# Two-layer graph network on one core: flags, carries and returned weights of the layer-0 softmax, and the split of 196 destination fetches

## What is computed

```python
edge_index = stack([src, dst])                    # 25000 edges, dst sorted; 100000 nodes, 64 features
h = maximum(layernorm(x), 0)
# layer 0, 4 heads
delta = proj[src] - proj[dst]                     # proj = h @ w_proj, per head
radial = delta . radial_score - scale * edge_weight
tangential = delta . tangential_score
out = sum over both of segment_sum(segment_softmax(logits, dst) * delta, dst)
x = x + h + nan_to_num(mean over heads of out) @ w_out
# layer 1, three rounds over x[row], x[col] with row = src, col = dst
mask = clip(sigmoid(MLP(x[row], x[col])) * 1.5 - 0.45, 0, 1)
vals = mask * d[row] * d[col]                     # d = clip(rowsum(mask) ** -0.5, 0, 10)
x_next = segment_sum(vals * x[col], row)
```

## Time and profile before

| | us |
|---|---|
| median of 3 runs | 2831.31 (2831.07 to 2831.59) |
| the profiled execution | 2831.4 |
| its span | 2829.6 |
| busy: PE / DVE / ACT / POOL | 1649.0 / 2091.3 / 1073.2 / 1905.7 |

### The profile page before, as it was taken

How to read it: one execution, slowest core, us unless ns; L and a number is a source line. 1 busy time by engine, 2 the same in 40 slices (tenths; PEclk the granted TensorE clock), 3 DMA queues, 4 the chain that set the end, 5 groups by cost and what they waited for, 6 DMA issues and landing times.

```text
span 2829.6 us, 32874 instructions
## 1 busy us (share of the span) xinstructions
PE 1649.0 (58%) x8788; PEld 1262.0 (45%) x8788; DVE 2091.3 (74%) x5660; ACT 1073.2 (38%) x2214; POOL 1905.7 (67%) x1896
## 2 busy tenths in 40 slices
PE   1135667676508888256666546746666655656663
PEld 0025666666405555145454334534444444434442
DVE  6766998899778999355655536979668889657775
ACT  0025666666304443033333334434444344442221
POOL 0037777777786766677777774767766477745776
PEclk9997877877558888577777767878888778876555
DMA  0023444444201111422222112333323333324443
GB/s 8 0 60 92 137 129 138 129 139 127 84 2 32 45 43 41 87 59 66 61 62 64 41 35 56 85 99 105 103 91 74 86 102 105 104 68 120 126 116 81
DMA packets 279791, 226.66 MB, mean 80 GB/s; under 512 B 161731, under 2 KB 209855, under 8 KB 279481
## 3 DMA queue, kind: packets, MB, share of 16 engines
q1 hardware_dynamic: 221113, 184.48, 23.1%
q0 software_dynamic: 58496, 40.08, 6.8%
HBM read 151.81 MB, written 84.50 MB: 84 GB/s over the span
## 4 chain that ended last, share of the span: by engine, by line
POOL 48%; DVE 18%; issue 18%; PE 7%; DVEq 6%; DMA 2%; SPq 1%; ACT 1%; POOLq 0%; ACTq 0%
POOL big L1096 14%; POOL G L1076 13%; POOL regs L1973 7%; POOL out L1103 7%; POOL regs L1982 6%; DVE den L1377 2%; DVE big L1706 2%; PE bank L1562 2%; DVE bank L836 2%; DVE big L1394 2%; DVEq L1705 1%; PE bank L994 1%; DVE bank L847 1%; DVE G L830 1%; DVEq L837 1%
## 5 line engine op out<-in xcount | busy, mean ns | idle before, releaser
L1096 POOL DMA_INDIRECT big<-layer_rows,late x392 | 401.0, 1023 | 152.0 <-issue 118.8
L1973 POOL DMA_INDIRECT regs<-in_x,G x200 | 202.2, 1011 | 234.8 <-DVEq L1825 174.2
L1562 PE MATMUL bank<-regs,SQ 99*128 99x256 bf16 x1308 | 228.7, 345 | 84.7 <-ACT SQ L1467 78.1
L1103 POOL DMA_INDIRECT out<-G,scat_i x196 | 195.7, 999 | 104.3 <-issue 61.6
L1982 POOL DMA_INDIRECT regs<-in_x,G x200 | 220.1, 1101 | 65.4 <-issue 60.3
L685 POOL DMA_INDIRECT x_after_layer<-big,scat_i x200 | 196.5, 983 | 84.3 <-issue 65.7
L1076 POOL DMA_INDIRECT G<-x_after_layer,own_i x196 | 199.9, 1020 | 70.2 <-issue 60.7
L1076 POOL DMA_INDIRECT G<-x_after_layer,far_i x196 | 197.8, 1009 | 65.8 <-issue 65.8
L1064 POOL DMA_INDIRECT late<-degree_factors,late x152 | 152.8, 1005 | 99.9 <-DMA degree_factors<-den 56.6
L1562 PEld LDWEIGHTS bank<-regs,SQ 99*128 99x128 bf16 x1308 | 153.9, 121 | 144.7 <-ACT SQ L1467 97.0
L439 PE MATMUL bank<-regs 128*128 128x128 f32 x784 | 135.9, 327 | 119.4 <-DVE den L397 118.7
(11 more groups left out here) (417 smaller groups left out, 5384.6 us busy)
## 6 DMA issues: line engine op xcount, KB each, us to landing
den<-in_x SPq DMA_DIRECT2D x96, 256.0 KB, 3.7
x_after_layer<-den SPq DMA_DIRECT2D x96, 256.0 KB, 2.1
regs<-x_after_layer SPq DMA_DIRECT2D x96, 256.0 KB, 2.8
out<-regs SPq DMA_DIRECT2D x96, 256.0 KB, 2.1
XC<-row_of_far_degree SPq DMA_DIRECT2D x109, 128.0 KB
layer_rows<-TS SPq DMA_DIRECT2D x98, 128.0 KB
regs<-sought SPq DMA_DIRECT2D x49, 196.0 KB
regs<-row_of_edge SPq DMA_DIRECT2D x75, 128.0 KB
```

The source lines that it names most:

```text
L1096: ahead(g, l, REVERSED, lambda u, l=l: g.indirect_dma_start(far[:, tile_of(u // C, u % C), :], None, xt_d[l - 1], bass.IndirectOffsetOnAxi ...
L1103: g.indirect_dma_start(out, bass.IndirectOffsetOnAxis(ap=scat_i[1][:, u:u + 1], axis=0), SUM[b][:, k, :], None, bounds_check=top, oob_is_e ...
L1562: ins = pe.matmul(bank[2 + 2 * b + k // 2][:, (k % 2) * 256:(k % 2) * 256 + 256], OH[b][0:RB1 + 1, k * P:(k + 1) * P], TAB[0:RB1 + 1, part ...
L1973: g.indirect_dma_start(GR[:, c % DEEP, k, 0, :], None, a["x"], bass.IndirectOffsetOnAxis(ap=own0[:, c * C + k:c * C + k + 1], axis=0), bou ...
```

## The change

It does the following:

- The flags "same node as the edge before" are stored as bf16 at the time of the sort (`run_d`, in place of the node numbers `node_d`) and loaded into `SAME` by one transfer, which SP issues before step 45 of the pairs. DVE makes `NEG`, the two end flags and the "whole partition is one run" flag (now a minimum) after the last pairs and before the last `scored`.
- The carries across partitions go through PE: columns are turned into rows by products with the identity, the row of carries back into columns by products with a 1x1.
- The 13 transposes and 26 DVE operations for the weights become 26 f32 products, accumulated in pairs, and two DVE copies.
- FETCHED is 20: 80 dst fetches on POOL and 29 look-ups, spread over the first 48 steps by `seeks`; `SQD` has two buffers. The cast of all 196 columns is on DVE after the loop.

```diff
+SPAN = NCH - 2
+PADS = (TS16 - T) * TE
-FETCHED = 24
+FETCHED = 20
-        NTROW = 128 + TS16 * 128 + 128
-        node_d = dram("tile_nodes", (2, NTROW))
+        run_d = dram("run_flags", (1, TS16 * TE + 1), BF16)
-        SAME = regs[:, 0:SCAN + 1]
+        SAME = regs[:, 1024:1024 + SCAN // 2 + 1].bitcast(BF16)[:, 0:SCAN + 1]
...
             for c in range(NCH):
+                if c == NCH - 5:
+                    sp.wait_ge(signal("g_own"), 40)
+                    sp.dma_start(SAME, at(run_d, 0, [[0, H8], [SCAN, HC], [1, SCAN + 1]])).then_inc(signal("scan_ids"), 16)
                 look_sp(sp, c + AHEAD + 2)
...
-            for h in range(H8):
-                rows = slice(h * HC, (h + 1) * HC)
-                sp.dma_start(IDS[rows, 1:SCAN + 1].rearrange("c (k e) -> c k e", k=KC),
-                             at(node_d, 128, [[KC * 128, HC], [128, KC], [1, TE]])).then_inc(signal("scan_ids"), 16)
-                sp.dma_start(IDS[rows, 0:1], at(node_d, TE - 1, [[KC * 128, HC], [1, 1]])).then_inc(signal("scan_ids"), 16)
-                sp.dma_start(IDS[rows, SCAN + 1:SCAN + 2], at(node_d, 128 + KC * 128, [[KC * 128, HC], [1, 1]])).then_inc(signal("scan_ids"), 16)
-            for n_ in range(2):
-                sp.wait_ge(signal("ends_up"), n_ + 1)
-                sp.dma_start(crow[0:1, 0:640], ccol[:, 0:5]).then_inc(signal("ends_row"), 16)
-                sp.wait_ge(signal("carry_row"), n_ + 1)
-                sp.dma_start(ccol[:, 5:7], carr[0:1, 0:256]).then_inc(signal("carry_col"), 16)
...
+        def seeks(c):
+            return range(min(c, SPAN) * len(LOOKED) // SPAN, min(c + 1, SPAN) * len(LOOKED) // SPAN)
...
         def row_carry(v, n_, is_max):
-            v.wait_ge(signal("ends_row"), 16 * (n_ + 1))
             v.memset(O, first)
-            v.tensor_tensor(A_[:, 0:m], lp[:, 1:128], full[:, 0:m], ALU.mult)
-            v.tensor_tensor(A2_[:, 0:m], ln_[:, 0:m], full[:, 1:128], ALU.mult)
+            v.tensor_copy(FULLR, full)
+            v.drain()
+            v.tensor_tensor(A_[:, 0:m], lp[:, 1:128], FULLR[:, 0:m], ALU.mult)
+            v.tensor_tensor(A2_[:, 0:m], ln_[:, 0:m], FULLR[:, 1:128], ALU.mult)
+            v.wait_ge(signal("ends_row"), n_ + 2)
...
-                v.tensor_tensor(B_[:, 0:m], lp[:, 1:128], last[:, 0:m], ALU.mult)
-                v.tensor_tensor(B2_[:, 0:m], ln_[:, 0:m], frst[:, 1:128], ALU.mult)
+                v.tensor_copy(B_[:, 0:m], lp[:, 1:128])
+                v.tensor_copy(B2_[:, 0:m], ln_[:, 0:m])
+                v.drain()
+                v.tensor_tensor(B_[:, 0:m], B_[:, 0:m], last[:, 0:m], ALU.mult)
+                v.tensor_tensor(B2_[:, 0:m], B2_[:, 0:m], frst[:, 1:128], ALU.mult)
...
-            v.wait_ge(signal("carry_col"), 16 * (n_ + 1))
+            v.wait_ge(signal("carry_col"), n_ + 1)
+            v.tensor_copy(ccol[:, 5:7], bank[2][:, 256:258])
+            v.drain()
...
+            v.wait_ge(signal("scan_ids"), 16)
+            v.tensor_copy(ccol[:, 2:3], SAME[:, 0:1])
+            v.tensor_copy(ccol[:, 3:4], SAME[:, SCAN:SCAN + 1])
+            v.tensor_reduce(ccol[:, 4:5], SAME[:, 1:SCAN], AX.X, ALU.min)
+            v.tensor_scalar(NEG, SAME, -1.0, -LOW, ALU.add, ALU.mult)
+            v.drain().then_inc(signal("ends_up"), 1)
             scored(NCH - 1)
...
-            v.wait_ge(signal("scan_ids"), 16 * 24)
-            v.tensor_tensor(SAME, IDS[:, 1:SCAN + 2], IDS[:, 0:SCAN + 1], ALU.is_equal)
-            v.tensor_tensor(ccol[:, 4:5], IDS[:, 1:2], IDS[:, SCAN:SCAN + 1], ALU.is_equal)
-            v.drain()
-            v.tensor_scalar(NEG, SAME, -1.0, -LOW, ALU.add, ALU.mult)
-            v.tensor_copy(ccol[:, 2:3], SAME[:, 0:1])
-            v.tensor_copy(ccol[:, 3:4], SAME[:, SCAN:SCAN + 1])
-            v.drain()
+            run_stored(v, RUN_A)
             v.wait_ge(signal("sm_in"), 4)
+            v.wait_ge(signal("ends_row"), 1)
...
-            for q in range(4):
-                n_ = min(4, KC - 4 * q)
+            for q, n_ in enumerate((8, KC - 8)):
                 v.wait_ge(signal("sm_back"), q + 1)
-                B = bank[4 + q % 2][0:TE, 0:n_ * P].rearrange("p (k r h c) -> p k r h c", r=2, h=HEADS, c=HC)
-                for k in range(n_):
-                    v.tensor_copy(BTv[0:TE, 4 * q + k], B[:, k, 0])
-                v.drain()
-                for k in range(n_):
-                    ins = v.tensor_tensor(BTv[0:TE, 4 * q + k], BTv[0:TE, 4 * q + k], B[:, k, 1], ALU.add)
-                ins.then_inc(signal("alpha_out"), 1)
+                B = bank[4 + q][0:TE, 0:n_ * F].rearrange("p (k h c) -> p k h c", h=HEADS, c=HC)
+                v.tensor_copy(BTv[0:TE, 8 * q:8 * q + n_], B)
...
+            pe.wait_ge(signal("ends_up"), 1)
+            for k in range(3):
+                ins = pe.matmul(bank[7][0:1, k * P:(k + 1) * P], ccol[:, 2 + k:3 + k], ident[:, :], start=True, stop=True)
+            ins.then_inc(signal("ends_row"), 1)
             pe.wait_ge(signal("sm_lg"), 1)
...
+            for n_ in range(2):
+                pe.wait_ge(signal("ends_up"), n_ + 2)
+                for k in range(2):
+                    ins = pe.matmul(bank[2][0:1, k * P:(k + 1) * P], ccol[:, k:k + 1], ident[:, :], start=True, stop=True)
+                ins.then_inc(signal("ends_row"), 1)
+                pe.wait_ge(signal("carry_row"), n_ + 1)
+                for k in range(2):
+                    ins = pe.matmul(bank[2][:, 256 + k:257 + k], carr[0:1, k * P:(k + 1) * P], ident[0:1, 0:1], start=True, stop=True)
+                ins.then_inc(signal("carry_col"), 1)
...
             for k in range(KC):
-                q = k // 4
-                if q >= 2 and k % 4 == 0:
-                    pe.wait_ge(signal("alpha_out"), q - 1)
-                ins = pe.transpose(bank[4 + q % 2][0:TE, (k % 4) * P:(k % 4 + 1) * P], SLk[:, k, :], ident[:, :])
-                if k % 4 == 3 or k == KC - 1:
+                o_ = bank[4 + k // 8][0:TE, (k % 8) * F:(k % 8 + 1) * F]
+                pe.matmul(o_, SLk[:, k, :], ident[:, 0:F], start=True, stop=False)
+                ins = pe.matmul(o_, SLk[:, k, :], SWAP[:, 0:F], start=False, stop=True)
+                if k in (7, KC - 1):
                     ins.then_inc(signal("sm_back"), 1)
...
-            for k in range(RING):
-                g.wait_ge(signal(f"ring{k}"), rows_in(k))
-            g.tensor_copy(far_i[:, 0:C * FETCHED], farf[:, 0:C * FETCHED])
-            g.drain().then_inc(signal("dst_done"), 1)
```

More of the change, by code:

```diff
@@ L629, in L0_sp @@
                     mask(c + 2)
-                if c % 2 == 0:
-                    seek_dst_sp(sp, c // 2 + 2)
+                for e in seeks(c):
+                    seek_dst_sp(sp, e + 2)
         WHELD = 32
@@ L700, in row_carry @@
         def row_carry(v, n_, is_max):
-            R = crow[0:1, 0:640].rearrange("o (q k) -> o q k", k=5)
-            last, frst, lp, ln_, full = [R[:, :, k] for k in range(5)]
+            last, frst = [bank[2][0:1, k * P:(k + 1) * P] for k in range(2)]
+            lp, ln_, full = [bank[7][0:1, k * P:(k + 1) * P] for k in range(3)]
             m = 127
@@ L863, in L0_dve @@
                     renew(i - 4)
-                if i >= 2 and i % 2 == 0 and i // 2 - 1 < len(LOOKED):
-                    seek_dst_dve(v, i // 2 - 1)
+                for e in seeks(i - 2) if i >= 2 else ():
+                    seek_dst_dve(v, e)
             v.drain()
-            lo = C * FETCHED
-            v.tensor_copy(far_i[:, lo:], farf[:, lo:])
+            for k in range(RING):
+                v.wait_ge(signal(f"ring{k}"), rows_in(k))
+            v.tensor_copy(far_i[:, :], farf[:, :])
             v.drain().then_inc(signal("dst_looked"), 1)
@@ L918, in L0_act @@
                 out_t(c)
-                if c % 2 == 0 and c // 2 < len(LOOKED):
-                    seek_dst_act(s_, c // 2)
+                for e in seeks(c):
+                    seek_dst_act(s_, e)
         def L0_pe(pe):
@@ L1006, in seek @@
             def seek(c):
-                if c % 2 == 0 and c // 2 < len(LOOKED):
-                    seek_dst_pe(pe, c // 2)
+                for e in seeks(c):
+                    seek_dst_pe(pe, e)
             staged(NCH, [(0, turn_weighed), (1, project), (3, out_proj), (2, seek)])
@@ L1186, in L1_dve @@
             v.drain().then_inc(signal("weights1_clear"), 1)
-            v.wait_ge(signal("dst_done"), 1)
             v.tensor_scalar(far_c, farf[:, :], 2.0, 1.0, ALU.mult, ALU.add)
@@ L1631, in _ @@
             sp.dma_start(at(rowe_d, 0, [[128, HT], [HT * 128, 2], [1, 128]]), EHR).then_inc(signal("row_out"), 16)
-            sp.dma_start(at(node_d, 128, [[128, HT], [HT * 128, 2], [1, 128]]), NTt[:, 0:2, :]).then_inc(signal("nodes_out"), 16)
+            sp.dma_start(at(run_d, 1, [[TE, HT], [HT * TE, 2], [1, TE]]), SM0[:, :, 0:TE]).then_inc(signal("nodes_out"), 16)
             sp.dma_start(at(same0_d, 1, [[128, HT], [HT * 128, 2], [1, 128]]), SM0).then_inc(signal("nodes_out"), 16)
```

(6 more changed lines are left out.)

15 lines of the change are left out of this document (7 added, 8 removed).

## The result

| | before | after |
|---|---|---|
| median, runs side by side on one chip | 2831.19 (2829.57 to 2833.05), 6 runs | 2822.15 (2816.32 to 2825.63), 6 runs |
| the profiled execution | 2831.4 | 2822.59 |
| its span | 2829.6 | 2820.7 |

The ratio is 0.9966 [0.9953, 0.9979]: faster by 9.0 us [5.9, 13.3]. The forecast was 2823.6 within 2818 to 2830, faster.

The account below looks back on a forecast made before the run. DVE was taken as the bound: when it begins the loop and how much it does there, with POOL catching up. Terms -10.2 - 3.0 - 2.1 + 4.1 - 1.5 + 4.0 + 1.0 = -7.7 gave 2823.6, range 2818 to 2830.

Parts of the forecast that it names:

- Flags early: Softmax before the loop: one early load replaces 24, so the first scan starts at 774.3, not 784.45: -10.2 us.
- Carries by PE: Softmax scans: first carry 4.5 us against 7.5 (-3.0), second 4.25 against 6.4 (-2.1).
- Halves added by PE: Weights turned back to tiles before the loop: 52 records where there were 13, 10.6 us against 6.5: +4.1.
- where the clock rises: 3.7 to 9.6 us of work: PE's 26 products: clock rises after that much work; the middle, 6.7, makes 27 records slow and 25 fast.
- the clock stays low to the loop: Rival: PE's clock stays low through the products (+6.8, no gain at the loop's start): -3.5 in all, 2827.9; chance 0.20.
- A warm PE at the loop's start: First two loop steps: if the products leave the clock high, their transposes run faster: -1.5 us (0 to -2.0).
- The look-ups: Loop: four more look-ups for sixteen fetches add +4.0 us of DVE work and +1.0 of waits (-3 to +8).
- the +1.0: Loop: DVE's added waits for PE from four more look-ups, at 0.43 us each, PE's idle being filled.
- falls less often in the loop: Rival: clock rises early (products +2.8) and falls less often as look-ups fill PE's gaps (waits -3): -13, 2818.4; chance 0.18.
- parts 4 and 5: Loop: -1.5 us from a warm PE at its start, and +4.0 work and +1.0 waits from four more look-ups.
- 16 fetches fewer on POOL: POOL before the scatters: free 20.8 us earlier, but its first rows come later than that, so worth nothing.
- priced each pass as a whole transpose: Rival for the 26 products: each f32 product costs four transposes, 25.6 us, +7.8 in all, 2839.2; chance 0.02.

Follow-up runs that it names:

- g5_loadlate: The changed kernel with the one load of flags issued after the last dense stores and the mask made after the logits' copy: 2826.87, ratio 0.9979 to before.
- f10_dmacarry: The changed kernel with the carries across partitions by transfers again, as in the kernel before: 2832.96, ratio 0.9991 to before.
- f3_turned: The changed kernel with 13 transposes again instead of 26 f32 products, DVE copying and adding groups of four tiles: 2818.92, ratio 0.9945 to before.
- f9_only_lookups: The kernel before with only the split changed, 80 fetches and 29 look-ups over 48 steps: 2834.40 against 2835.03, ratio 0.9995.
- g7_best20: f3_turned with the mask made after the logits' copy: 2818.87, ratio 0.9944 to the kernel before.
- f1_even24: The changed kernel with its split undone, 96 fetches and 25 look-ups, one in every second step: 2826.06, ratio 0.9972 to before.

## Why the prediction was right, and where it was not

The sum was near and the direction right, though two of its terms were missed, in ways that nearly cancel.

1. *Flags early: right.* From the last operation of the pairs to the first scan 22.42 became 12.24, the 10.2 of the forecast. The minimum took 1.85 (1.8 forecast) and the mask 1.00 (1.01). The heading "flags early" names the lesser half: g5_loadlate and SP's queue show that 8.1 of it is one transfer for 24, and 2.1 the early issue.

2. *Carries by PE: right.* 4.57 and 4.29 against 4.5 and 4.25; the trip back waits 1.13, where the earlier trace rows have 0.94 and 1.1 was taken. Undone in f10_dmacarry: 4.7.

3. *Halves added by PE: right sign, size missed.* From the end of the division to the copy for the weighing (L822) 6.51 became 12.33: +5.8, not +4.1. The step that failed is "where the clock rises: 3.7 to 9.6 us of work". It was read from the loop, and here 52 records back to back held the engine 11.35 of 11.40 us at a granted 0.50 to the end. The reading of 3.7 also began its count at 855.90 and left out what PE had done just before it. Between 847.40 and 852.2 it worked 3.56 us on the 13 transposes, these being the last five:

```profile
850.23 1.12 PE L973 MATMUL bank<-ident,regs 128*126 128x128 f32 x4 [0.86 <-DVE den L817]
851.75 0.47 PE L973 MATMUL bank<-ident,regs 128*126 128x128 f32 x1 [0.41 <-DVE den L817]
```

All 13 were slow, and so were the loop's first two groups behind them (1.97 and 1.89 for eight). The rival "the clock stays low to the loop" was right for this part. Its price of +6.8 was high, since a record took 0.2135 here, where the rows have 0.246, and that for records of 128 and of 64 columns alike; these runs don't show why. The low-clock case was given 0.20, too little. The 0.50 of the earlier trace rows did not speak strongly for it, as PE had nothing to do in those two stretches; the slow transposes of the very stage that was to change did.

4. *A warm PE at the loop's start: failed.* -1.5 was forecast; the way from the first weighing to the first scan over segments went from 7.03 to 8.16, +1.1. The first two groups of transposes are slow and so is the first L1003 in its greater part (3.01, where the next take 1.93). The clock rose only at about 851, some 6 us after the loop's first transpose. From that transpose to the first group of eight at the high clock it is 5.5 to 6.7 us with the 26 products ahead (six kernels) and 5.4 to 6.4 with 13 transposes ahead (before, f3_turned, f9_only_lookups, g7_best20). So the products' work brought the rise no earlier.

5. *The look-ups: cost right, waits wrong.* DVE's work rose by 3.7 (4.0 forecast). The waits were to rise by 1.0 and fell from 10.8 to 3.6. The step that failed is the +1.0, taken from the mean wait for each look-up as if waits came with look-ups. They come with slow spells of PE's clock: of the 10 waits before, 9 stand within 5 us behind a slow group of w_out products, in f1_even24 all 8, in the change 3 of 4. And those spells are fewer with 29 look-ups: the second half of the rival "falls less often in the loop" was right, its first half (clock early) false. Together the loop gave -1.4 from first weighing to last scatter, where parts 4 and 5 were to give +3.5.

6. *16 fetches fewer on POOL: nothing, right.* POOL waits for DVE 44.2 us in the change, and f1_even24, with the 16 fetches back and the four look-ups gone, has a ratio within 0.0006 of the change's.

7. *Not foreseen:* the last scores came 0.5 earlier than before in spite of the mask, since the pairs ended 1.5 earlier. No part of the change bears on that. Over all these kernels the last scores start between 763.5 and 768.7, so it lies within the scatter between executions and chips.

The balance on the trace: -1.5 (pairs) - 10.2 - 3.0 - 2.1 (carries) + 5.8 (products) + 0.4 (a gap of issue of 0.43 between the second scan and the end copies, and roundings) makes -10.6 at the first weighing; -1.4 in the loop; +3.0 of scatter after it: -9.0, against the 8.9 that the span shows. That the forecast came within 1.5 us of the measured median is in part luck. At the first weighing it had -11.2 where -10.6 was measured, and 1.5 of that is scatter of the pairs. The loop came out 4.9 better than forecast (-1.4, not +3.5), and the 3.0 of scatter behind it hid part of that.

On the f32 product, the Trainium skill ("FP8 and Floating Point Precision", TensorE Precision Notes) says that true FP32 takes four passes. The prediction priced each pass as a whole transpose; the trace shows 0.427 a product, less than two of the low clock's transposes (0.246 each), so that price falls. Counted in columns it is the other way round: 0.427 × 1200 / 64 is 8.0 cycles for each column, where four passes of one cycle each (an estimate from that rule of the Trainium skill) would be four. PEld, the weight load, is busy 11.16 of the 11.40 us, and a record of 64 columns (0.2135) is hardly shorter than one of 128 (0.234 in f3_turned). So it seems that the weight loads, two to a product, fill the time and the columns hide in them; no run varied the columns alone to show it. For 512 columns the rule of the Trainium skill does nearly fit:

```profile
860.63 1.90 PE L1003 MATMUL bank<-den,wm 128*64 128x512 f32 x4
```

Two products, 1.90 at the high clock: 0.95 × 2400 / 512 is 4.45 cycles for each column.

**What stays open.** Why four more look-ups keep the clock up when 25 moved apart hardly do. From the first weighing to the last scatter PE's idle times of 1.9 us and more are 14 in the change and 15 before, so the longest gaps are not what went. Look-ups alone (f9_only_lookups) gain 3.4 in the loop and show nothing in the total. In its trace the last scores come 3.7 later than before, but that is another chip, where they start at 765.2 to 768.7 in all four kernels; a gain of 3.4 in whole times is below what its interval can tell. What PE's weight loads have to do with the 0.50 during the products is not tried either. Not tried: 13 f32 products with the sum of identity and SWAP as the moving matrix, which would add the halves in 26 records, 5.6 us by the 0.2135 measured, still more than the 3.04 of the transposes, though with two copies instead of eight operations on DVE.

## What to carry to other kernels

Price PE's work in a stretch of low granted clock as low to its end, unless a row of that same stretch shows a rise: here 26 products took 11.4 us of it, and the way to the loop was 6.4 shorter with 13 transposes and eight copies and adds on DVE. Where an engine waits for many small transfers of one array, first count them and read the issuing engine's queue: 24 transfers took SP 13.6 us to issue, one in their place gave 8.1, and issuing it early only 2.1 more. And a change of several parts should be undone part by part: here one of its parts cost 6 us of the 15 that two others brought.

## What was not expected of the hardware

- 52 f32 records back to back, 11.35 us busy of 11.40, left the granted clock at 0.50; the loop's mixed work raised it some 6 us after its start.
- 24 transfers on SP's queue went out 0.57 us apart, 13.6 us in all, and DVE went on 1.9 us behind the last.
- The loop's clock goes with the number of look-ups: 0.84 and 0.85 with 25, 0.89 to 0.91 with 29, 0.90 with 33. DVE's waits for them fall from 8.6 to 10.8 down to 2.1 to 5.1 us.
- One load of 128 rows of 3.3 KB took 6.1 us from issue to use after the pairs (g5_loadlate), with the dense rows' stores already landed and only POOL's fetches beside it.
- The 9.62 us of issue before the first scatter came when POOL made the cast (0.26 us) and its drain just before it. With the same 96 fetches and the cast on DVE (f1_even24) 0.30 was left. Nothing here shows what it is. It cost nothing, as POOL catches up with DVE either way.
